# Attention scores of a decoder block: 64 keys of two groups per stationary operand, and two masks issued before the maxima's transposition

## The reference

```python
q = (Q @ w_q.T).reshape(B, S, G, HG, HD)
k = (K @ w_k.T).reshape(B, S, G, HD)
v = (V @ w_v.T).reshape(B, S, G, HD)
scores = jnp.einsum('bnghd,bmgd->bnghm', q, k) / scale
scores = jnp.where(causal, scores, NEG_INF)
attn = jax.nn.softmax(scores, axis=-1)
out = jnp.einsum('bnghm,bmgd->bnghd', attn, v).reshape(B, S, D)
```

## Time and profile before

| | us |
|---|---|
| three runs | 515.18, 515.73, 516.11 |
| median | 515.73 |
| span of the profiled execution, first to last instruction | 513.8 |
| PE, DVE, ACT, POOL busy in it | 457.6, 378.6, 318.1, 327.8 |

### The profile page before, as it was taken

The page is one execution under the profiler, slowest core; times in us unless marked ns, Lnnn a source line. Parts: engine busy times, 40 slices in busy tenths (PEclk is TensorE's granted clock), DMA queues, the critical chain, the costliest instruction groups (busy, mean ns, idle before and its releaser), DMA issues.

```text
span 513.8 us, 12310 instructions
## 1 busy us (share of the span) xinstructions
PE 457.6 (89%) x3120; PEld 391.6 (76%) x3120; DVE 378.6 (74%) x1854; ACT 318.1 (62%) x869; POOL 327.8 (64%) x473
## 2 busy tenths in 40 slices
PE   3779999999999999999978999899999999989920
PEld 2567777887877787877756998799999999879910
DVE  4355688888778988777986886556565657998986
ACT  2367687777787777787736565556565656555520
POOL 4111347777677777777676777777766677756770
PEclk9989999999999999999999999999999999999985
DMA  7232535862323222321227669999655669999775
GB/s 199 81 130 74 166 118 180 229 193 93 107 91 105 105 87 93 104 93 75 74 86 242 201 232 295 315 292 290 218 158 143 204 197 339 357 307 318 262 259 190
DMA packets 52261, 93.79 MB, mean 183 GB/s; under 512 B 9974, under 2 KB 41246, under 8 KB 52002
## 3 DMA queue, kind: packets, MB, share of 16 engines
q1 hardware_dynamic: 37346, 46.11, 31.1%
q0 software_dynamic: 12240, 32.14, 16.7%
q10 hardware_dynamic: 2608, 14.76, 8.5%
HBM read 53.61 MB, written 43.41 MB: 189 GB/s over the span
## 4 chain that ended last, share of the span: by engine, by line
PE 47%; DVE 22%; DMA 9%; SPq 8%; issue 7%; ACT 5%; POOL 2%; POOLq 0%; DVEq 0%; ACTq 0%
PE bank L1411 9%; DVE NM L789 7%; PE bank L1443 6%; PE bank L1104 6%; DMA pool_a<-rows 4%; DVE NM L791 4%; PE bank L1245 4%; PE bank L1287 3%; PE bank L1362 3%; SPq L361 3%; SPq L366 3%; PE bank L1261 3%; PE bank L1166 2%; PE bank L1433 2%; PE bank L1099 2%
## 5 line engine op out<-in xcount | busy, mean ns | idle before, releaser
L469 POOL DMA_INDIRECT rows<-rowb,idx x112 | 110.9, 990 | 55.0 <-DVE rowb L889 28.3
L1411 PE MATMUL bank<-wgu_sb,PT 128*128 x572 | 105.0, 327 | 0.9 <-ACT PT L496 0.9
L1411 PEld LDWEIGHTS bank<-wgu_sb,PT 128*128 128x128 f32 x572 | 91.3, 190 | 1.0 <-issue 1.0
L479 POOL DMA_INDIRECT parts<-PT,dst_all x72 | 72.0, 1000 | 29.8 <-issue 22.6
L496 ACT ACTIVATE PT<-bank 128x512 f32<-128x512 f32 x108 | 61.6, 593 | 27.8 <-PE bank L1443 19.3
L1443 PE MATMUL bank<-wd_sb,VC 96*128 x286 | 73.6, 379 | 0.0
L589 ACT ACTIVATE PT<-bank 128x512 f32<-128x512 f32 x96 | 53.7, 619 | 5.7 <-PE bank L1261 5.7
L998 DVE SCALAR_TENSOR_TENSOR PT<-PT,bank 128x192 f32<-128x192 f32 x72 | 25.2, 349 | 41.1 <-ACT PT L623 41.0
L1443 PEld LDWEIGHTS bank<-wd_sb,VC 96*128 96x128 f32 x286 | 52.2, 190 | 4.0
L623 ACT ACTIVATE PT<-bank 128x192 f32<-128x192 f32 x72 | 23.7, 329 | 45.4 <-PE bank L1411 45.4
L496 ACT ACTIVATE Q<-bank 9x256 fp32r<-9x256 f32 (+1 forms) x96 | 42.5, 443 | 11.4 <-PE bank L1240 9.7
(11 more groups left out here) (270 smaller groups left out, 1142.8 us busy)
## 6 DMA issues: line engine op xcount, KB each, us to landing
pool_a<-rows SPq DMA_DIRECT2D x96, 148.5 KB
qN<-rows SPq DMA_DIRECT2D x47, 148.5 KB
wgu_sb<-wgu_d SPq DMA_DIRECT2D x8, 768.0 KB, 5.2
rows<-pad SPq DMA_DIRECT2D x33, 152.0 KB
pool_a<-parts ACTq DMA_DIRECT2D x5, 896.0 KB, 7.1
KA<-parts ACTq DMA_DIRECT2D x5, 896.0 KB
Q<-parts ACTq DMA_DIRECT2D x5, 896.0 KB
wd_sb<-wd_d SPq DMA_DIRECT2D x2, 1536.0 KB, 11.3
```

Source lines behind the costliest of these rows:

```text
L469: gp.indirect_dma_start(out=rows, out_offset=bass.IndirectOffsetOnAxis(ap=idx[b % 2][:, k:k + 1], axis=0), in_=rowb[b % 2][:, :], in_offse ...
L479: gp.indirect_dma_start(out=parts, out_offset=bass.IndirectOffsetOnAxis(ap=dst[q % NDST][:, j:j + 1], axis=0), in_=yb[q % FEED][:, j, :], ...
L1411: last = t.matmul(GU_PS[q % 2][:, j * 2 * NI:(j + 1) * 2 * NI], xTb[q % 2][:, j, k * P:(k + 1) * P], wgu_sb[:, k, one_of(expert[i]), :].sq ...
```

## The change

The upper queries' scores are taken in the form that the lower queries' had: `KA` is laid out by half of the keys, then by group, so that 64 keys of two groups lie next to each other. `s0`, `s1` are upper keys with upper queries (masked), `s2`, `s3` lower keys with upper queries (no mask, the products start the bank), `s4`, `s5` lower keys with lower queries (masked). `KL`, `causTr` and the POOL step `kL` are gone. `sm` issues two masks and stands before `c` in PE's order. The values lie in `vaL` and `vaU`, with four copies of 64x32; `pv0` has eight products, `pv1` four. Setup counts of semaphores follow (`setup_g`, `vl`). Left out below are those counts, the name lists and the step table.

```diff
@@ -54,7 +53,7 @@
-           "c": 32.9, "sm": 34.4, "s0": 34.5, "s1": 35.6, "s2": 36.1, "s3": 36.6, "s4": 36.8, "s5": 37.6, "pv0": 38.9, "pv1": 40.2,
+           "sm": 32.5, "c": 32.9, "s0": 34.5, "s1": 35.6, "s2": 36.1, "s3": 36.6, "s4": 36.8, "s5": 37.6, "pv0": 38.9, "pv1": 40.2,
@@ -65,7 +64,7 @@
-    "POOL": {"r1": -12, "r4": -2.2, "r7": 3.9, "r13": 17.4, "kL": 29.5, "r17": 46.3, "wo": 51.5, "xT": 60, "sc0": 74.6, "sc1": 77.4, "sc2": 80.5,
+    "POOL": {"r1": -12, "r4": -2.2, "r7": 3.9, "r13": 17.4, "r17": 46.3, "wo": 51.5, "xT": 60, "sc0": 74.6, "sc1": 77.4, "sc2": 80.5,
@@ -180,13 +179,11 @@
-        KA = [KA_all[:, p * NG * P:(p + 1) * NG * P].rearrange("p (g m) -> p g m", g=NG) for p in range(2)]
-        va, vaL = two("va", [P, 2 * VP]), two("vaL", [P, P])
-        va_g = [v[:, :].rearrange("p (n w) -> p n w", n=2)[:, :, 0:P].rearrange("p n (k c) -> p n k c", c=32) for v in va]
-        vaL_g = [v[:, :].rearrange("p (k n c) -> p n k c", n=2, c=16) for v in vaL]
+        KA = [KA_all[:, p * NG * P:(p + 1) * NG * P].rearrange("p (a g m) -> p a g m", a=2, g=NG) for p in range(2)]
+        vaL, vaU = two("vaL", [P, P]), two("vaU", [P, P])
+        vaL_g, vaU_g = ([v[:, :].rearrange("p (k n c) -> p n k c", n=2, c=16) for v in u] for u in (vaL, vaU))
...
-        KL = sb("KL", [P, NG * H], f32r)
@@ -392,14 +389,13 @@
-                gp.memset(va[p][:, :], 0.0).then_inc(S["setup_g"], 1)
+                gp.memset(vaU[p][:, :], 0.0).then_inc(S["vl"], 1)
...
-                pool.wait_ge(S["vl"], 3 * p + 1)
+                pool.wait_ge(S["vl"], 6 * p + 2)
...
+                    gp.memset(vaU_g[p][n * H:n * H + H, n, :, HD:HD + 1], 1.0).then_inc(S["vl"], 1)
...
-                    pool.wait_ge(S["vl"], 3 * p + 2 + n)
-                pool.wait_ge(S["setup_g"], 12 + 4 * p)
-                gp.memset(va_g[p][:, :, :, HD:HD + 1], 1.0).then_inc(S["setup_g"], 1)
+                    pool.wait_ge(S["vl"], 6 * p + 4 + 2 * n)
@@ -434,12 +430,6 @@
-
-            def kL(b):
-                pool.wait_ge(S["KA"], nth("KA", b))
-                if b > 0:
-                    pool.wait_ge(S["s"], nth("s", b - 1, 6))
-                gp.tensor_copy(KL[0:MR, :].rearrange("p (g m) -> p g m", g=NG), KA[b % 2][0:MR, :, 0:H]).then_inc(S["kl"], 1)
@@ -552,14 +542,12 @@
-                    act.wait_ge(S["setup_g"], 19)
+                    act.wait_ge(S["vl"], 12)
...
-                copy(va_g[b % 2][:, :, :, 0:HD], o[:, GD:2 * GD].rearrange("p (k n d) -> p n k d", n=2, k=4))
-                if b == 0:
-                    act.wait_ge(S["vl"], 6)
-                for n in range(2):
-                    last = copy(vaL_g[b % 2][n * H:n * H + H, n, :, 0:HD], o[0:H, GD:2 * GD].rearrange("p (k n d) -> p n k d", n=2, d=HD)[:, n, :, :])
+                for half, v in enumerate((vaL_g, vaU_g)):
+                    for n in range(2):
+                        last = copy(v[b % 2][n * H:n * H + H, n, :, 0:HD], o[half * H:half * H + H, GD:2 * GD].rearrange("p (k n d) -> p n k d", n=2, d=HD)[:, n, :, :])
@@ -569,7 +557,7 @@
-                    last = ac.activation(KA[b % 2][0:MR, g, :], o[0:MR, hf * P:(hf + 1) * P], ACT.Copy, scale=own8[0:MR, g:g + 1])
+                    last = ac.activation(KA[b % 2][0:MR, :, g, :], o[0:MR, hf * P:(hf + 1) * P].rearrange("p (a m) -> p a m", a=2), ACT.Copy, scale=own8[0:MR, g:g + 1])
@@ -706,7 +694,6 @@
-                v.tensor_copy(causTr[:, :], causalT)
@@ -1221,16 +1208,16 @@
-                    keys = KA[b % 2][0:KR, HG * hf:HG * hf + HG, :]
+                    keys = KA[b % 2][0:KR, :, HG * hf:HG * hf + HG, :]
...
-                        t.matmul(o[:, :], queries(b, 1, pair), keys.rearrange("p g m -> p (g m)"), start=True, stop=False)
+                        t.matmul(o[:, :].rearrange("p (g a m) -> p g a m", g=HG, a=2), queries(b, 1, pair), keys.rearrange("p a g m -> p g a m"), start=True, stop=False)
...
-                            last = t.matmul(o[:, 2 * P * n:2 * P * (n + 1)].rearrange("p (g m) -> p g m", g=HG), queries(b, 0, n), keys[:, :, 0:H], start=False, stop=n == 1)
+                            last = t.matmul(o[:, 2 * P * n:2 * P * (n + 1)].rearrange("p (g m) -> p g m", g=HG), queries(b, 0, n), keys[:, 0, :, :], start=False, stop=n == 1)
@@ -1241,56 +1228,49 @@
 
             def masked(i, b):
                 o = ring(f"s{i}", b)
-                later = causTr[:, H:] if i < HG else causLr[:, :]
-                t.matmul(o[:, :].rearrange("p (a n) -> p a n", n=H), nident[:, :], later.unsqueeze(1).to_broadcast([P, 2 * HG, H]),
+                t.matmul(o[:, :].rearrange("p (a n) -> p a n", n=H), nident[:, :], causLr[:, :].unsqueeze(1).to_broadcast([P, 2 * HG, H]),
                          start=True, stop=False)
                 return o
 
             def first_masks(b):
-                for i in range(3):
+                for i in range(2):
                     masked(i, b)
 
-            def upper(i):
-                hf, kind = i // 2, i % 2
+            def scores(i):
+                hf, queries, keys = i % 2, int(i < 4), int(i < 2)
 
                 def f(b):
-                    o = ring_bank(f"s{i}", b) if i < 3 else masked(i, b)
+                    o = ring_bank(f"s{i}", b) if i < 2 else ring(f"s{i}", b) if i < 4 else masked(i, b)
                     if i == 0:
                         pe.wait_ge(S["Q3c"], nth("Q3c", b, 1))
+                    elif i == 4:
+                        pe.wait_ge(S["Q3c"], nth("Q3c", b, 2))
                     for u in range(2):
-                        last = t.matmul(o[:, 2 * P * u:2 * P * (u + 1)].rearrange("p (h n) -> p h n", h=HG), KA[b % 2][0:MR, HG * hf + 2 * kind + u, :],
-                                        Q2[b % 2][0:MR, hf, 1, :, :], start=False, stop=u == 1)
+                        g = HG * hf + 2 * u
+                        last = t.matmul(o[:, 2 * P * u:2 * P * (u + 1)].rearrange("p (h n) -> p h n", h=HG), KA[b % 2][0:MR, keys, g:g + 2, :].rearrange("p g m -> p (g m)"),
+                                        Q2[b % 2][0:MR, hf, queries, :, :], start=u == 0 and 2 <= i < 4, stop=u == 1)
                     last.then_inc(S["s"], 1)
                 return f
 
-            def lower(hf):
-                def f(b):
-                    o = masked(HG + hf, b)
-                    if hf == 0:
-                        pe.wait_ge(S["kl"], nth("kl", b))
-                        pe.wait_ge(S["Q3c"], nth("Q3c", b, 2))
-                    for u in range(2):
-                        last = t.matmul(o[:, 2 * P * u:2 * P * (u + 1)].rearrange("p (h n) -> p h n", h=HG), KL[0:MR, P * (2 * hf + u):P * (2 * hf + u + 1)],
-                                        Q2[b % 2][0:MR, hf, 0, :, :], start=False, stop=u == 1)
-                    last.then_inc(S["s"], 1)
-                return f
-
             def pv(n):
                 out4 = V_PS[:, :].rearrange("p (h n) -> p h n", h=HG)
+
+                def values(b, first, v, at, start, stop):
+                    for k in range(4):
+                        flat_p = PT[:, first + k // 2, :, :].rearrange("p h n -> p (h n)")
+                        last = t.matmul(out4[32 * k:32 * k + 32, :, at:at + H], v[b % 2][:, 32 * k:32 * k + 32],
+                                        flat_p[:, 2 * P * (k % 2):2 * P * (k % 2 + 1)].rearrange("p (h n) -> p h n", h=HG), start=start, stop=stop)
+                    return last
 
                 def f(b):
                     if n == 0 and b > 0:
                         pe.wait_ge(S["vc"], nth("vc", b - 1))
                     pe.wait_ge(S["e"], nth("e", b, 4 + 2 * n))
-                    for k in range(4):
-                        at, flat_p = P * n + 32 * k, PT[:, k, :, :].rearrange("p h n -> p (h n)")
-                        last = t.matmul(out4[32 * k:32 * k + 32, :, H:], va[b % 2][:, at:at + 32],
-                                        flat_p[:, 2 * P * n:2 * P * (n + 1)].rearrange("p (h n) -> p h n", h=HG), start=n == 0, stop=False)
-                    if n == 1:
-                        for k in range(4):
-                            flat_p = PT[:, HG + k // 2, :, :].rearrange("p h n -> p (h n)")
-                            last = t.matmul(out4[32 * k:32 * k + 32, :, 0:H], vaL[b % 2][:, 32 * k:32 * k + 32],
-                                            flat_p[:, 2 * P * (k % 2):2 * P * (k % 2 + 1)].rearrange("p (h n) -> p h n", h=HG), start=False, stop=True)
+                    if n == 0:
+                        values(b, 0, vaU, H, True, False)
+                        last = values(b, 2, vaL, H, False, False)
+                    else:
+                        last = values(b, 4, vaL, 0, False, True)
                     last.then_inc(S["pv"], 1)
                 return f
 
```

More of the change, by code:

```diff
@@ L21 @@
 VW = 66
-VP = P + 16
 NTOK = NB * P
@@ L148, in decoder_kernel @@
         iota_k, tok8 = cob[:, at0 + 4:at0 + 4 + TOP], cob[:, at0 + 4 + TOP:]
-        nident, identr, causalr, causTr = (sb(n, [P, P], f32r) for n in ("nident", "identr", "causalr", "causTr"))
```

(13 more changed lines are left out.)

## The result

| | before | changed |
|---|---|---|
| median of the runs compared | 514.55 us (20 runs) | 520.97 us (20 runs) |
| ratio, changed to before | | 1.0124 [1.0099, 1.0149] |
| profiled execution: time, span | span 513.8 us | 522.89 us, span 521.1 us |
| one steady period | 15.30 us | 15.73 us |

The change makes the kernel slower by 1.24%, some 6.4 us. The forecast was +2.5 us. Medians here are of all executions, while ratios and their intervals take the fast ones alone, with the kernel before timed again beside each experiment, so a ratio can differ from the quotient of two medians (experiment 1: 517.24 against 513.65, ratio 1.0011).

What follows compares the result with a forecast made beforehand. No single engine but a loop through PE, DVE and ACT was the bound. Thirteen periods +3.0, first two blocks' copies +0.6, block 0 −1.0, causTr −0.1: +2.5 on 515.73 gives 518.2 us, range 511.8 to 520.8.

Steps and rivals of the forecast that it cites:

- the bank wait: Before `c` on PE: a moved mask waits for its bank until ACT's eight KA copies end; `c` +0.56.
- The start: Before block 0's `mx0`: first two blocks' copies cost +0.6, the dropped causTr copy gives −0.1.
- the expert phase is moved as a whole: After the blocks: the expert phase only shifts in time, put at 0 for itself.
- The masks ahead of `c`: Two masks queued before `c` on PE: `c` ends at 221.42, not 220.86, +0.56 a block.
- Fewer masks after `c`: From `c` to first value products: PE has 0.92 less, but ACT's Q copies and exponentials end last; −0.63 a block.
- Value products: Between `c` and `r7`: same number, four move ahead of `r16`, `r17` may wait some 0.1; cost 0, uncovered 0.1.
- Value copies: ACT between `r7` and `r9`: four 64x32 copies replace three; without overlap first copy to qkT grows 0.53 to 0.84, +0.30.
- The rest: POOL's dropped cast, later statistics and KA written in two runs: 0; DVE's dropped causTr copy at the start: −0.1.
- Rival (C): ACT's KA copies: two runs cost 0.02 for each of eight, `c` 0.16 later, +2.1 in all: 520.3; chance 0.10.
- (A): Masks before `c` not held by KA copies: `c` loses 0.1, a block −0.23, total 511.9; chance 0.13.
- (D): (A) and (B) together: −0.48 for each of thirteen blocks and −1.3, total 508.2; chance 0.04.
- (B): ACT's value copies overlap, +0.05 to +0.1: a block ±0, total 514.5 to 515.2; chance 0.20.

Runs made afterwards that it cites:

- experiment 1: Changed kernel with its two masks issued behind `r13` again: median 517.24 us, ratio to before 1.0011.
- experiment 2: Changed kernel with PE's `kT` issued before `mx3` and not behind it: median 512.30 us, ratio 0.9982.
- experiment 3: Kernel before, with two of its six masks put ahead of `c` and nothing else changed: 521.89 us, one execution.
- experiment 9: Changed kernel without ACT's two copies that fill vaU: 515.20 us, one execution.
- experiment 4: Kernel before, with two more 64x32 ACT copies from lower to upper partitions behind the value copies: 514.80 us, one execution.
- experiment 5: Changed kernel with its four value copies reordered, those writing the same partition half side by side: 521.52 us, one execution.
- experiment 11: Changed kernel with POOL's cast of KA kept in its old place, though nothing reads it: 520.23 us, one execution.
- second pair: Both kernels unaltered, profiled a second time: changed kernel 520.92 us, kernel before 515.94 us.
- experiment 6: Changed kernel with `kT` issued before `mx3` and value copies ordered by the partitions they write: median 511.23 us, ratio 0.9968.

## Why the prediction failed by its size

The direction held, and so did the main mechanism, the bank wait; 520.97 lies just outside the range. The failed steps are sizes. A steady block, forecast at +0.23, measured +0.43, and half of that miss is the step from the exponentials to the value products (0.04 put, 0.14 measured). The start, put at +0.5, measured −1.1. And "the expert phase is moved as a whole" was not borne out: it measured 3.9 and 1.1 us longer, for a cause that stays open. The terms, in their order:

**The masks ahead of `c`.** Right. The bank of `s0` is held by the KA copies, and `c` ends 0.60 later (forecast 0.56); experiments 1, 2 and 3 show it by taking it away twice and making it once. The step "the bank of `s0` is the one that `kT` of the next block used last, in every block from 0 to 14" is wrong for block 0: the ring gives that bank to `s1` there, and the second mask waits, not the first (PE's timeline):

```profile
31.92 0.49 PE L1231 MATMUL bank<-causLr,nident 128*128 128x512 f32 x1
32.98 0.50 PE L1231 MATMUL bank<-causLr,nident 128*128 128x512 f32 x1 [0.56 <-ACT KA L560]
```

`c` of block 0 so ends 4.91 after its `mx0` for 4.82, late by 0.09 and not by 0.28, and the period from its `mx0` to the next is 1.07 shorter (forecast 0.77, of the −1.0 and the +0.23).

**Fewer masks after `c`.** The step "only then, in its order, the first four exponentials" was right, and its size was off: −0.53, not −0.63. From ACT's last exponential to PE's value products the chain shows 0.14, where I had put 0.04 from the issue before `r9`. That is the 0.10.

**Value products.** "Cost 0" hid a delay. `r17` was to wait some 0.1; it waits for DVE's qN, comes 0.53 after the start of `r7` for 0.27 before, and pushes `r8` back: 1.36 after `r7`'s end for 1.15. The timelines of DVE and PE in the changed kernel:

```profile
119.04 0.48 DVE L754 SCALAR_TENSOR_TENSOR qN<-bank,scalars,qN 128x256 fp32r<-128x256 f32 x1 [0.17 <-ACT qN L529]
...
119.67 0.53 PE L1180 MATMUL bank<-identr,qN 128*96 128x128 f32 x4
```

In the changed kernel the four copies cover most of it, and 0.04 shows: the Q copy after `r17` starts 0.55 after the end of `r7`, for 0.51 when it followed ACT's v_sb. Without the vaU copies (experiment 9) `r7` to `r9` is 0.10 longer than before, the price that the prediction had put on a lost cover.

**Value copies.** The price of "if none of these overlaps" was nearly right: first copy to qkT 0.81 to 0.84 for 0.53. The reason given was wrong, as experiments 4 and 5 show: partition 64 is not what forbids the overlap. So the right size was in part luck. Taken out, the two vaU copies are worth 0.19 and not the full 0.31, since the late `r8` stands close behind them.
The Trainium skill, ScalarE: Activation LUTs, section What ACT_TABLE_LOAD costs, has neighbours overlap by about 93 ns. The two probe copies agree with it: each lasts 0.18 and they start some 0.09 apart. The four copies of the changed kernel don't: each lasts 0.19 and they start 0.19 to 0.21 apart.

**The rest.** POOL's cast at 0: right, by experiment 11. KA in two runs of 64 at 0: right, 2.14 to 2.17 for eight as in the earlier trace rows. Rival (C) falls with it.

**The sum.** A steady block is +0.43 instead of +0.23: 0.04 for the masks, 0.10 for the exponentials, 0.06 on ACT's path to `r9`. Over thirteen periods these errors make +2.6. The span by stretch, changed less before, in the first and the second pair of profiles (rounded):

| stretch, us | forecast | first pair | second pair |
|---|---|---|---|
| start to `mx0` of block 0 | +0.5 | −1.1 | −1.1 |
| from there to `c` of block 13 | +2.0 | +4.2 | +4.5 |
| from there to `c` of block 15 | 0 | +1.2 | +1.0 |
| from there to the first expert product | 0 | −0.8 | −0.5 |
| from there to the end of the span | 0 | +3.9 | +1.1 |
| sum | +2.5 | +7.3 | +5.0 |

The start went the other way, and that hid most of the error of the steady blocks. The copies there did cost their 0.6: the first copy to qkT is 0.70 in blocks 0 and 1, for 0.45 and 0.41. But the first transfer landed 0.75 and 0.83 earlier in the two pairs, and from its landing to DVE's first `chat` it is 5.1 for 5.9 in both pairs, where −0.1 for causTr was put. Where the rest of that 0.8 comes from was not tried, and the start scatters: `mx0` of block 0 starts from 28.39 to 30.11 in profiles with the changed kernel's setup.

Two more things go beyond the sum:
- Block 14 to 15 takes 18.12 for 16.90. Half of that is the masks again. PE is late there, and both stand ahead of `c` after DVE's last maxima, which end at 272.63 (PE's timeline):

```profile
272.70 0.82 PE L1231 MATMUL bank<-causLr,nident 128*128 128x512 f32 x2
273.36 0.27 PE L1227 MATMUL bank<-con,NM 128*128 128x128 f32 x1
```

Where the other half comes from was not tried. Part of it is given back by the 0.8 in the table, since the chain of that block runs through POOL's statistics and `rowb`, not through `c`.
- The periods 9 to 10 and 12 to 13 last 16.10 and 16.29, with DVE waiting for a transfer to land:

```profile
DVE rowb L683 <- DMA rows<-rowb,idx: 1.2, 2, 0.8
```

The kernel before has one long period, 16.63, from block 1 to 2, where the changed kernel has 15.89. These vary from run to run (15.96 and 15.89 for the first two when the changed kernel ran again, 15.91 for the last when the kernel before did).

The first product of the expert phase starts 3.4 us later than before (282.0 for 278.6), 3.9 in the second pair (281.1 for 277.2). "The expert phase is moved as a whole" then leaves 2.5 to 3.0 of the 6.4 us to be found behind it. From that product to the end of the span the changed kernel took 239.1 and 238.0 us, the kernel before 235.2 and 236.9. But experiments 1, 5 and 9, with the same expert phase as the changed kernel, took 236.8, 236.3 and 233.4. This stretch scatters by more than the difference. Whether the change costs anything there, and by which transfers, stays open.

The rivals: (A) and (D) fall, since `c` ends 5.36 after the start of `mx0`, some 1.03 after DVE's last maxima. (B) falls, since the copies don't overlap. That masks ahead of `c` cost 0.1 or less when their banks are free, as (A) had it, fits experiment 2. Its gain of 0.23 a block doesn't: with the banks free the period is 0.11 below that of the kernel before, and the statistics path holds it.

## What to carry to other kernels

Before an instruction is moved forward in an engine's order, look up who last read the buffer that it writes: work that is nearly free behind a wait costs the whole wait when it is queued ahead of it. A wait taken on a loop of three engines shows up at full price, while work saved on the engine that is busiest ends where the next engine is late; here 0.92 us less PE work after `c` gave 0.53. Price small neighbouring copies by the spacing of their starts, for the very pair of partitions that they read and write.

## What the runs showed of the hardware

- Small ACT copies overlap or not by what they touch; this fits every pair that was read, and the column gaps were not taken apart from it. A 64x32 copy after one that reads and writes the same partition halves starts some 0.09 us after it (the probes of experiment 4, behind a vaL copy of the same kind). Where the half read or the half written changes between lower and upper, it starts 0.19 to 0.21 after, which is the full duration of the copy ahead. Both matter: with only the read half changed vaU follows vaL at 0.20 in experiment 5 (122.53 to 122.73), with only the written half changed the second vaU follows the first at 0.21 in the changed kernel (121.29 to 121.50).
- From ACT's end to PE's start the chain shows 0.04 before `r9` and before the masks, but 0.14 before the value products, in every period read.
- The statistics of DVE and POOL were hidden by little: with the period at 15.19 PE already waits for them in 8 blocks (experiment 2), in 9 in experiment 6.
